# Turning the row maxima one slot later, behind the value products, in a windowed-attention and expert-mixture kernel

## The reference

```
q = heads(concat([ctx, layernorm(x)]) @ Wq)             # 32 heads of 16
k, v = heads(layernorm(x) @ Wk), heads(layernorm(x) @ Wv) # 8 heads, each for 4 of q
ssm_k, ssm_v = heads(ctx @ Wsk), heads(ctx @ Wsv)
scores = q @ concat([ssm_k, k]).T / 4 + alibi            # masked to the last 64 positions
o = softmax(scores) @ concat([ssm_v, v])
x = x + tanh(g_xattn) * (o @ Wo)
```

## Time and profile before

| | us |
|---|---|
| median of 3 runs | 873.09 (870.61 to 874.34) |
| the profiled execution | 872.62 |
| its span in the profile | 870.6 |
| PE matmul busy | 858.4 (99%) |
| DVE busy | 545.2 (63%) |
| ACT busy | 399.3 (46%) |
| POOL busy | 519.9 (60%) |

### The profile page before, as it was taken

The page is one execution under the profiler, slowest core; times in us unless marked ns, Lnnn a source line. Parts: engine busy times, 40 slices in busy tenths (PEclk is TensorE's granted clock), DMA queues, the critical chain, the costliest instruction groups (busy, mean ns, idle before and its releaser), DMA issues.

```text
span 870.6 us, 17391 instructions
## 1 busy us (share of the span) xinstructions
PE 858.4 (99%) x6662; PEld 753.4 (87%) x6662; DVE 545.2 (63%) x984; ACT 399.3 (46%) x807; POOL 519.9 (60%) x532
## 2 busy tenths in 40 slices
PE   9899999999999999999999999999999999999998
PEld 8889999999999998988888877888888888888886
DVE  7675666766666657756446756556655655665567
ACT  5754545554545544655035243444444444444431
POOL 3861443535335232343769998548888887888641
PEclk9999999999999999999999999999999999999999
DMA  8678676776868659630101354320212022021046
GB/s 275 170 143 180 152 207 186 191 196 167 205 165 218 163 139 256 144 100 25 49 25 49 102 168 157 134 73 25 82 40 73 25 72 73 25 84 38 1 151 236
DMA packets 76509, 108.09 MB, mean 124 GB/s; under 512 B 7274, under 2 KB 47979, under 8 KB 75403
## 3 DMA queue, kind: packets, MB, share of 16 engines
q1 hardware_dynamic: 74168, 105.94, 43.4%
q10 hardware_dynamic: 2258, 1.03, 0.5%
HBM read 70.71 MB, written 31.00 MB: 117 GB/s over the span
## 4 chain that ended last, share of the span: by engine, by line
PE 84%; POOL 10%; DMA 2%; DVE 2%; issue 1%; SPq 1%; ACT 0%; POOLq 0%; ACTq 0%
PE ps_scores L2227 20%; PE ps_proj L1846 15%; PE ps_scoresT L2227 10%; PE ps_scoresT L1983 7%; PE ps_o L1997 6%; PE ps_scores L1956 5%; PE ps_proj L2227 5%; PE ps_proj L1904 5%; PE ps_scores L1846 3%; PE ps_proj L1835 3%; PE ps_scoresT L1846 1%; DMA q_stack<-max_rows 1%; POOL sum_lo L953 1%; POOL sum_raw L968 1%; POOL sum_raw L966 1%; DMA xn_rows<-in_x 1%
## 5 line engine op out<-in xcount | busy, mean ns | idle before, releaser
L1128 ACT ACTIVATE probsT<-ps_scoresT 128x512 f32<-128x512 f32 (+1 forms) x256 | 138.9, 545 | 148.9 <-PE ps_scoresT L1983 144.4
L1490 DVE TENSOR_REDUCE neg_max<-ps_scores 128x2 f32<-128x384 f32 (+1 forms) x256 | 131.6, 516 | 108.6 <-PE ps_scores L1956 107.8
L1357 ACT ACTIVATE part_sums<-ps_scores 128x512 f32<-128x512 f32 x96 | 57.4, 598 | 130.1 <-PE ps_scores L2227 130.0
L1983 PE MATMUL ps_scoresT<-q_stack,k_stack 116*128 116x256 f32 x448 | 106.1, 307 | 0.8 <-DMA q_stack<-max_rows 0.8
L841 POOL TENSOR_TENSOR o_normal<-o_blocks,inv_sums 128x256 f32<-128x256 f32 x32 | 19.9, 622 | 138.0 <-DVE inv_sums L1511 138.0
L1956 PE MATMUL ps_scores<-k_stack,q_stack 114*128 114x192 f32 (+1 forms) x512 | 94.5, 267 | 2.7 <-DMA q_stack<-qT_hi 1.6
L1956 PEld LDWEIGHTS ps_scores<-k_stack,q_stack 114*128 114x128 f32 x512 | 83.0, 190 | 9.5 <-DMA q_stack<-qT_hi 2.3
L996 POOL TENSOR_TENSOR w_expert_lo<-w_sums,w_expert_hi 128x256 fp32r<-128x256 f32 x64 | 64.2, 1014 | 44.9 <-ACT w_expert_hi L1277 44.9
L1008 POOL TENSOR_TENSOR big<-big,basis 128x512 f32<-128x512 f32 x56 | 77.9, 1409 | 16.3 <-DVE basis L1785 16.3
L1983 PEld LDWEIGHTS ps_scoresT<-q_stack,k_stack 116*128 116x128 f32 x448 | 70.8, 190 | 4.7 <-DMA q_stack<-max_rows 1.0
L1776 DVE TENSOR_TENSOR basis<-part_sums,silu_gate 128x512 f32<-128x512 f32 x32 | 24.2, 755 | 67.3 <-ACT silu_gate L1365 67.3
(11 more groups left out here) (309 smaller groups left out, 2500.9 us busy)
## 6 DMA issues: line engine op xcount, KB each, us to landing
k_stack<-k_kept SPq DMA_DIRECT2D x64, 192.0 KB, 4.3
big<-coeff_rows SPq DMA_DIRECT2D x8, 1024.0 KB, 4.8
q_stack<-q_kept SPq DMA_DIRECT2D x40, 192.0 KB, 4.1
q_kept<-qT_hi SPq DMA_DIRECT2D x10, 512.0 KB
x_rows<-in_x SPq DMA_DIRECT2D x9, 512.0 KB, 5.8
k_kept<-kT_hi SPq DMA_DIRECT2D x16, 256.0 KB
x_kept<-x_rows SPq DMA_DIRECT2D x16, 256.0 KB, 2.6
w_raw<-in_L_ffn_w_gate SPq DMA_DIRECT2D x16, 256.0 KB, 2.8
```

Of the source, the lines that this page charges most:

```text
L1128: act.activation(PT[:, g % 2, 2 * j:2 * j + blocks].rearrange("p h f r w -> p (h f r w)"), ST[:, n % 2, 0:blocks].rearrange("p h n -> p (h ...
L1357: act.activation(TP[:, u % 2, j, :], src[:, u % 2, :], ACT.Copy).then_inc(taken, 1)
L1490: dve.tensor_reduce(NM[:, g // 2 % 2, g % 2, 2 * i:2 * i + 2], SA[:, n % 2, :, 0:keys], AX.X, ALU.max, negate=True).then_inc(max_done, 1)
L1983: ins = pe.matmul(ST[:, n % 2, v, :], KS[0:ROWS, g, j + v, 1 - v].rearrange("p w s -> p (w s)"), QS[0:ROWS, g, j + v].rearrange("p f r w - ...
```

## The change

The turn of the maxima moves from slot 8p + 9 to slot 8p + 10, on TensorE and on ScalarE. The transfer into the stack moves from slot 8p + 10 to 8p + 11. On ScalarE the copy goes ahead of its slot's exponentials instead of behind them. The wait of the turn for the exponentials is that of the unit which now last wrote `PM`'s bank.

```
-MAX_HALVES, NM_TURN, STACK_MAX = PAIR, PAIR + 1, PAIR + 2
+MAX_HALVES, NM_TURN, STACK_MAX = PAIR, PAIR + 2, PAIR + 3
...
-            if LAG <= n < END + LAG:
-                exponentials(n - LAG)
             p = pair_due(n, NM_TURN)
             if p is not None:
                 max_out(p)
+            if LAG <= n < END + LAG:
+                exponentials(n - LAG)
...
             pe.wait_ge(nm_lo, p + 1)
-            if unit >= 2:
-                pe.wait_ge(exp_done, unit - 1)
+            if unit >= 3:
+                pe.wait_ge(exp_done, unit - 2)
             elif p >= 1:
                 pe.wait_ge(nm_out, p)
```

## The result

The changed kernel took 877.51 us in the median of 7 runs (876.2 to 878.63); the kernel before took 872.74 us in the median of 7 beside it (870.61 to 874.34). The ratio is 1.0058, with a 95% interval of 1.0041 to 1.0075: slower, by a little more than the 0.5% that the prediction took as the least that can be told, and its interval holds that bound. As a change it is +4.8 us, where +2.5 was forecast. The profiled executions have 876.59 and 872.62 us, and spans of 874.6 and 870.6 us.

What follows compares the result with a forecast made beforehand. TensorE's own instruction stream, busy 858.4 of 870.6 us, was taken to bound the kernel. The terms -2.9 + 2.0 - 0.8 + 3.0 + 1.2 gave +2.5 us, a median of 875.6 us, range 870 to 880.

Steps and rivals of the forecast that it cites:

- the turn leaves, with the waits that go: Slot 8p + 9 on TensorE: removing the turn saves 0.09 us each, and waits in pairs 28 and 30 save 0.8 us.
- the turn behind the value products: Slot 8p + 10 on TensorE: the turn costs 0.06 us in thirty pairs, between 0.026 and 0.09, together +1.8 us.
- N waits for the copy: Slot 8p + 11: the turned scores (N) wait for ScalarE's copy, 0.1 us between bounds 0 and 0.2, 30 pairs, +3.0 us.
- transfer of pair 26: This pair's transfer of the maxima, issued 1.4 us later, lands later and TensorE waits: +1.2 us, ends 0 and 2.1.
- sign of being wrong: At N in slot 8p + 11: waits over 0.17 us per pair would show the prediction wrong.
- second rival: Slot 8p + 11: N pays a full round trip through ScalarE, 0.2 to 0.25 us per pair, 879.2 us at 0.22; chance 0.14.
- drain rule: TensorE: changing the tiling mode drains it; by this rule the turn's new place costs +1.0 us in place of +2.0.
- Pair 27: The turn's wait for the halves goes, but the first scores still wait for VectorE's reduction: no gain.
- pair 28: Scores to transposes, 0.80 us against the ordinary 0.44: a gain of 0.36 us as the turn leaves.
- pair 30: TensorE idled 0.27 us ahead of the turn; with weights exposed after a stall, a gain of 0.4 us.
- third rival: Later transfers fall behind SyncE's in several pairs and turned scores wait; two more waits of 1.5 us, 878.6; chance 0.09.
- first rival: The turn hides behind the value products, the copy is in time, pair 26 no later: -2.7 us, 870.4; chance 0.17.

Runs made afterwards that it cites:

- own_place: Changed kernel, but for pairs 2 to 30 the turn writes unused columns of a `ps_scores` bank, so N needs no wait for the copy; 870.33 us, ratio 0.9984.
- n_behind: Changed kernel with N issued behind the four transposes of slot 8p + 11 in the 14 pairs that have them; 873.76 us, ratio 1.0014.
- copy_behind: Changed kernel with ScalarE's copy put back behind the exponentials of its slot, the turn staying in its new slot; 900.32 us, ratio 1.0322.
- middle: Changed kernel with the turn between the two halves of the value products, except in pairs 0 and 1; 879.93 us, ratio 1.0089.
- plain: Changed kernel with the turn, still behind all value products, as an ordinary matmul with the identity in place of the transpose; 877.38 us, ratio 1.007.
- ahead: Changed kernel with the turn ahead of the value products in slot 8p + 10, waiting for the exponentials of unit 8p - 9; 874.59 us, ratio 1.0028.
- dve_copy: Changed kernel with VectorE in place of ScalarE copying the turned maxima, behind its maxima of the slot; 878.81 us, ratio 1.0074.
- own_place_again: The kernel of own_place run once more for its interval; 870.05 us, ratio 0.9983.
- stack_early: Changed kernel with the transfer of the maxima back in slot 8p + 10, the turn and the copy staying; 876.13 us, ratio 1.0052.
- middle_plain: Kernel of middle, with the turn as an ordinary matmul with the identity in place of the transpose; 875.32 us, ratio 1.0042.

## Why the prediction was right, and where it was not

The median came at 877.51, within the range of 870 to 880, 1.9 us over the 875.6 forecast. I gave 0.78 to a change within 0.5%, and it was 0.58%, just outside. Step by step, in us of the span, from the two traces:

| term | predicted | measured |
|---|---|---|
| the turn leaves, with the waits that go (pairs 2 to 30) | -3.4 | -2.6 |
| the turn behind the value products | +1.8 | +0.6 |
| N waits for the copy | +3.0 | +6.3 |
| transfer of pair 26 | +1.2 | -0.9 |
| start-up, last pair, rest | 0 | +0.5 |
| sum | +2.5 | +3.9 |

(The -3.4 is 29 x 0.09 and 0.8; the first and last pairs and rounding make the sum. The measured +0.6 is 29 x 0.02.)

**What failed: the size of N's wait.** The step was "I take 0.1, between the two, for 30 pairs: +3.0 us", with 0.2 as the upper bound. It measured 0.20 to 0.23 in every pair, which is over the 0.17 us that the prediction named as a sign of being wrong; own_place and n_behind took it away, and copy_behind moved it with the copy. The mechanism was right, and so were its first parts: the copy starts at T + 0.32 and ends at T + 0.59. Two readings were off. I took 0.05 us for the release and it took 0.11, behind either engine; rows 6 show a first wait, and N's for the copy is a second one. That made the load 0.22 us late, where I had 0.09 to 0.15. And I let the lateness be partly hidden: N's matmul came 0.16 us after its undisturbed time, and the next product another 0.06, so all 0.22 were paid. The rows for the second part were in hand (0.31 for 0.2 behind a stall); I had them in the text, and took half of it all the same. The second rival, with 0.22 us a pair, was the right mechanism at the right size, and had a chance of 0.14. Its lateness of 0.15 us at most, which spoke against it, was the wrong figure. Its sum, +6.1 us, came out over the measured +4.8 by the two terms that it shared with the forecast and that were too dear.

**The price of the new place** was 0.02 us, under the lower end of 0.026 to 0.09. The lower end stood there for a turn in the value products' mode. The turn isn't in it, as middle shows. It is cheap because the idle time between the value products and the next product of another mode is paid in any case: 0.11 us, by the 1.56 us of plain beside the 1.67 of the other two kernels. S paid it before, and now the turn pays and S follows after 0.04 us. The drain rule of the Trainium skill (TensorEngine Tiling (Array Packing), Key Properties) gave the nearer sum here; my sentence about which neighbours the turn shares its mode with was the wrong reason for it.

**What left the old place** was 0.08 us a pair, as read. Pair 27 gained nothing, as foretold, since the scores wait for their maxima there anyway; pair 28 gained 0.45 in its slot in this trace, but in those of own_place, ahead and dve_copy the same slot is 0.3 us longer than before, and in own_place_again, the same kernel as own_place, 0.45 shorter: such a single wait changes from one execution to the next; pair 30 did not gain the 0.4, since the next product then waits for `logitsT`. A wait on one engine's bound stream is worth its length only if nothing else is late just behind it.

**The transfer** cost nothing, where +1.2 us was forecast: no wait for pair 26's stands in the trace. stack_early puts it back and changes nothing that can be told. The third rival is out.

**The first rival,** that the gain arrives, did not happen, but its time did, once the wait was taken away: own_place took 870.33 and 870.05 us, beside its 870.4. As changes these are -1.8 and -1.4 us, where it had -2.7: part of the agreement is luck.

That the total came near is owed in part to errors that cancel: N's wait 3.3 us too small, against 1.2 and 2.1 us too much for the new place and the transfer.

## What to carry to other kernels

Where a result goes out to another engine and its buffer is wanted again, count the whole round trip (here 0.32 us to the copy, 0.27 for it, 0.11 back, read from a wait of the same kind) against what the waiting engine has between, and add what comes late behind the wait. If the trip is longer by a tenth of a microsecond, it is paid every time on the engine that bounds the kernel; give the result a buffer of its own, or put other work between, before moving the producer closer to its consumer. Measure such a wait by the distance of starts in matching slots of two traces, since neither the table of waits nor the busy share shows it. And a small product placed next to a change of TensorE's mode that is paid anyway was almost free here (0.02 us), while between two products of that mode it paid both ways (0.35).

## What the runs showed of the hardware that was not expected

- A transpose of 4-byte numbers with 32 columns of weights, between matmuls of 32 columns, made the slot 0.35 us longer, and 0.02 at their end.
- An ordinary matmul of the same numbers ran as two matmul instructions, each with a weight load of its own, 0.11 us apart (0.20 us for the turn in middle_plain and in plain). It had no idle time around it among the 32-column matmuls.
- The release of TensorE's weight load took 0.11 us behind the copy, from ScalarE and from VectorE, where that wait was the second of two, and 0.05 where it was the only one (unit 1 in copy_behind and dve_copy) or the first (the turn of pair 27). The reason is open.
- A wait of 0.22 us in each of 29 pairs, 6.3 us in all, stood in the table of waits as one of 0.2 us, and the whole change as 4.2 us more of busy time. The Trainium skill (Perfetto Trace Analysis, Tensor Engine Instruction) says that TensorE's end times are estimated from an instruction's size; this trace agrees, as the rows of 0.36 us ahead of N reach exactly to its start and are no longer than without the wait.
